# Cross-attention and mixture of experts: head stacks filled from tile to tile, the last residual added on TensorE, new due times

## The chip, the cores and the metric

The kernel runs on one core of one Trainium2 chip. The metric is the device time of one execution in microseconds. The median of three runs of the kernel before is 1670.79 us (1665.35 to 1675.45).

## The reference

Eight batches of 512 tokens, 512 features, 16 heads of 32. Layer norm, cross-attention to a context, a residual, a second layer norm, and a top-k mixture of eight experts in which each expert takes the 512 tokens with the highest probability for it. All in float32.

```python
def attn(q, k, v):                      # 8 x 512 x 512 each
    qh, kh, vh = heads(q @ Wq + bq), heads(k @ Wk + bk), heads(v @ Wv + bv)
    sim = einsum('bnid,bnjd->bnij', qh, kh) * 32 ** -0.5
    sim = where(mask, sim, lowest)
    return join(einsum('bnij,bnjd->bnid', softmax(sim), vh)) @ Wo + bo

x = x + attn(layernorm(x), ctx, ctx)
xf = layernorm(x).reshape(4096, 512)
route_prob = softmax(xf @ Ws + bs).T                 # 8 x 4096
route_vals, routes = top_k(route_prob, 512)
h = gelu(einsum('ekd,edf->ekf', xf[routes], W1) + b1)    # f = 2048
out = (einsum('ekf,efd->ekd', h, W2) + b2) * route_vals[..., None]
x = x + zeros.at[routes].add(out)
```

## The kernel before, in words

The attention part works on 32 groups g: batch b = g // 4 and four heads. Float32 products are made of fp32r ones, with every operand split into a hi and a lo half: hi·hi, lo·hi and hi·lo.

For a group, TensorE projects k and q: `proj` (L1855 to L1857), four times three matmuls for each of k and q, features on the partitions. ScalarE writes the hi half from PSUM (L1257, `qT_hi` or `kT_hi`, a tile of 128 partitions = 4 heads × 32 features, by 512 tokens), and VectorE the lo half (L1461).

The scores need another layout, the stack: 32 features of each head on partitions, the four heads side by side on the free axis, and hi, lo, hi (for q; hi, hi, lo for k) one under another, so that one matmul over 96 rows sums the three products. `kst` and `qst` are rings of NST = 3 stacks, a group uses slot g mod 3. The halves reach them through memory. SP issues `keep_hi` and `keep_lo` (L948, L955), each a store of 256 KB from the tile into `qk_rows`, and then `stack_hi` (L979, two transfers) and `stack_lo` (L990), which load it back as "(h d) s -> d h s". A stack's transfer waits for the store, and for the last score of group g − 3. The evacuation of the next projection, L1257 and L1461, waits for the store of the last. SP issues its transfers in one order of its own; a wait holds up all that stand behind it.

`max` (L1873) multiplies q by k for the row maxima, taken on VectorE (L1476), with the sum of exponentials on ScalarE (L1280). The maxima are transposed (`rows`, L1890) and become further rows of the stack (`by_row`, through POOL L1174). `score` (L1905) makes the scores once more, transposed, with the maxima subtracted; ScalarE exponentiates them into `p_ring` (L1292); `att` (L1916) multiplies by v, in fp32, four heads on 32 columns each. `rden` (L1897) and VectorE's L1508 divide; L1301 and L1532 split the result into `oT`.

For each tile t of 128 tokens of a batch, `outa` and `out` (L1932 to L1934) make the output projection of the first and the last two groups. In the last batch `out` is cut in two: `osum` with group 30, `out` with group 31, into the same bank. VectorE adds `outa` to x, then `out` (L1547), takes the statistics (L1380 to L1384), and normalises (L1389). `route` (L1944) transposes the result, `logits` (L1955) and `back` (L1963) make the router's values. From about 894 us the experts follow, which the change leaves alone.

Which step comes next on which engine is set before the program is written, by a planner (`attention_agenda`, class `Plan`). Every step has a due time (`at`, in groups; tables K_AT, Q_AT, MAX_AT, SPAN and others, plus LAG), a cost and the steps that must be ready. The planner plays the engines forward: on an engine, of the steps that can start within LOOK of the earliest, the one with the smallest due time goes. All seven general PSUM banks go by the same plan.

Of the kernel before, what the change touches and what calls it, by code (L numbers as in the profile page):

```python
# [371 lines left out]
LAG = {
    ("act", "proj"): 0.055, ("dve", "proj_lo"): 0.027, ("pool", "rows_lo"): -0.636, ("act", "rows"): 0.028, ("dve", "rows_lo"): -0.369,
    ("sync", "stack_hi"): -0.057, ("sync", "stack_lo"): 0.367, ("pool", "recip"): -0.231, ("dve", "rden"): -0.146, ("dve", "outa"): -0.826,
# [1776 lines left out]
```

## Time and profile before

| | before |
|---|---|
| median of three runs | 1670.79 us |
| the profiled execution | 1667.8 us |
| its span | 1666.0 us |
| mean granted clock of TensorE | 0.985 |
| TensorE busy (PE) | 1597.9 us, 96% |
| VectorE busy (DVE) | 1113.7 us, 67% |
| ScalarE busy (ACT) | 976.8 us, 59% |
| GpSimd busy (POOL) | 300.0 us, 18% |
| DMA, mean | 130 GB/s |

PE, DVE, ACT and POOL are TensorE, VectorE, ScalarE and GpSimd; SPq is SyncE's issue of transfers; PEld is the loading of weights, which runs beside PE. L1905 is line 1905 of the kernel. A row such as "out<-in" names what is written and what is read. The number in square brackets at a row's end is the time for which the engine stood idle before it, and what released it; "issue" is idle time for which the profile shows no wait. A matmul's own duration overlaps the next one's, so work is measured by the distance of the starts.

### The profile page before, as it was taken

The page shows a single profiled execution, that of the slowest core. Times are in us where ns is not written, and L with a number is a line of the kernel's source. Part 1 is how long each engine was busy: PE and PEld are TensorE (multiplying, and loading weights), DVE is VectorE, ACT ScalarE, POOL GpSimd, SP SyncE. Part 2 cuts the span into 40 slices and gives each one's busy share as a digit, 9 for nine tenths or more (in the row PEclk, how much of TensorE's full clock was granted, in tenths as well). Part 3 has the DMA queues.
Part 4 walks back from the last instruction along what each step waited for, and adds up shares of the span by engine and source line. Part 5 has one row for each costly group of instructions (what it writes and reads, how often), then busy time and mean ns, then how long its engine had stood idle before and what let it go on. Part 6 is the DMA issues. An engine that isn't in the chain of part 4 may idle for free.

```text
span 1666.0 us, 22367 instructions
## 1 busy us (share of the span) xinstructions
PE 1597.9 (96%) x7847; PEld 1162.0 (70%) x7847; DVE 1113.7 (67%) x1950; ACT 976.8 (59%) x2115; POOL 300.0 (18%) x396
## 2 busy tenths in 40 slices
PE   7999999999999999999886999999999999999997
PEld 5556666666666666666544787888888888888885
DVE  7676878878788797787746577765554555454543
ACT  5788898989989899798872223222222223232331
POOL 6220221302213022130300201002020202020110
PEclk9999999999999999999997999999999999999999
DMA  5643654626547364462611423416252524343330
GB/s 179 184 123 95 193 145 140 208 80 205 144 132 207 87 200 147 134 192 83 190 67 64 127 89 90 152 57 184 76 159 101 159 91 144 101 132 119 102 110 26
DMA packets 131271, 217.27 MB, mean 130 GB/s; under 512 B 17116, under 2 KB 51056, under 8 KB 131160
## 3 DMA queue, kind: packets, MB, share of 16 engines
q1 hardware_dynamic: 114520, 173.23, 33.1%
q0 software_dynamic: 16640, 42.61, 9.6%
q8 instruction: 63, 1.03, 0.3%
q14 instruction: 48, 0.39, 0.1%
HBM read 157.45 MB, written 57.82 MB: 129 GB/s over the span
## 4 chain that ended last, share of the span: by engine, by line
PE 86%; DVE 7%; ACT 2%; DMA 2%; issue 2%; POOL 0%; SPq 0%; DVEq 0%; POOLq 0%; ACTq 0%
PE ps_gen L888 9%; PE ps_gen L890 9%; PE ps_gen L889 9%; PE ps_gen L1905 7%; PE ps_gen L2069 7%; PE ps_gen L2071 7%; PE ps_gen L2070 7%; PE ps_gen L1873 7%; PE ps_att L1916 7%; PE ps_gen L1855 3%; PE ps_gen L1856 3%; PE ps_gen L1857 3%; PE ps_gen L1932 2%; PE ps_gen L1933 2%; PE ps_gen L1934 2%
## 5 line engine op out<-in xcount | busy, mean ns | idle before, releaser
L1476 DVE TENSOR_REDUCE nmax<-ps_gen 128x1 f32<-128x512 f32 x512 | 331.9, 684 | 79.5 <-PE ps_gen L1873 77.8
L1292 ACT ACTIVATE p_ring<-ps_gen,keep_scale 128x512 f32<-128x512 f32 x512 | 341.3, 702 | 44.2 <-PE ps_gen L1905 30.7
L1280 ACT ACTIVATE ps_gen<-ps_gen,nmax 128x512 f32<-128x512 f32 x512 | 342.6, 676 | 33.6 <-DVE nmax L1476 33.4
L1349 ACT ACTIVATE gel<-ps_gen,b_cols 128x512 f32<-128x512 f32 x128 | 88.3, 690 | 448.8 <-PE ps_gen L890 448.7
L1737 DVE TENSOR_TENSOR gel_lo<-gel,gel_hi 128x512 fp32r<-128x512 f32 x126 | 87.3, 692 | 281.6 <-ACT gel_hi L1350 277.3
L888 PE MATMUL ps_gen<-hT_hi,w_hi 128*128 128x512 f32 x512 | 202.2, 395 | 0.2 <-DVE hT_lo L1730 0.2
L1873 PE MATMUL ps_gen<-kst,qst 97*128 97x512 f32 x512 | 193.0, 424 | 8.6 <-issue 4.6
L890 PE MATMUL ps_gen<-hT_hi,w_lo 128*128 128x512 f32 x512 | 199.5, 390 | 0.0
L889 PE MATMUL ps_gen<-hT_lo,w_hi 128*128 128x512 f32 x512 | 199.4, 389 | 0.0
L1905 PE MATMUL ps_gen<-qst,kst 99*128 99x512 f32 x512 | 194.9, 424 | 3.8 <-DMA qst<-by_row 3.1
L2069 PE MATMUL ps_gen<-w_hi,gel_hi 128*128 128x512 f32 x504 | 198.1, 393 | 0.0
L2071 PE MATMUL ps_gen<-w_hi,gel_lo 128*128 128x512 f32 x504 | 196.5, 390 | 0.0
L2070 PE MATMUL ps_gen<-w_lo,gel_hi 128*128 128x512 f32 x504 | 196.3, 389 | 0.0
L1873 PEld LDWEIGHTS ps_gen<-kst,qst 97*128 97x128 f32 x512 | 95.4, 192 | 78.3 <-issue 50.0
L1905 PEld LDWEIGHTS ps_gen<-qst,kst 99*128 99x128 f32 x512 | 93.5, 190 | 78.2 <-issue 58.8
L1202 POOL DMA_INDIRECT out_x<-y_out,idx x28 | 49.6, 1770 | 511.1 <-ACT y_out L1369 504.7
L1916 PE MATMUL ps_att<-p_ring,v_sb 128*32 128x512 f32 x1024 | 138.4, 613 | 1.8 <-ACT p_ring L1292 1.6
L1280 ACT ACTIVATION_READ_ACCUMULATOR ps_gen<-ps_gen,nmax 128x1 f32 x512 | 113.8, 222 | 0.0
L890 PEld LDWEIGHTS ps_gen<-hT_hi,w_lo 128*128 128x128 f32 x512 | 96.1, 188 | 20.5
L888 PEld LDWEIGHTS ps_gen<-hT_hi,w_hi 128*128 128x128 f32 x512 | 96.1, 188 | 19.6 <-issue 0.5
L889 PEld LDWEIGHTS ps_gen<-hT_lo,w_hi 128*128 128x128 f32 x512 | 96.2, 188 | 19.3
L2071 PEld LDWEIGHTS ps_gen<-w_hi,gel_lo 128*128 128x128 f32 x504 | 94.6, 188 | 19.8
(218 smaller groups left out, 2672.0 us busy)
## 6 DMA issues: line engine op xcount, KB each, us to landing
w_raw<-in_L_ffn_W SPq DMA_DIRECT2D x128, 512.0 KB, 3.3
kst<-qk_rows SPq DMA_DIRECT2D x93, 256.0 KB, 4.0
qst<-qk_rows SPq DMA_DIRECT2D x93, 256.0 KB, 4.1
x_in<-in_x POOLq DMA_DIRECT2D x60, 256.0 KB, 4.1
out_x<-x_in SPq DMA_DIRECT2D x32, 256.0 KB, 3.3
qk_rows<-kT_hi SPq DMA_DIRECT2D x31, 256.0 KB, 2.3
qk_rows<-kT_lo SPq DMA_DIRECT2D x31, 256.0 KB, 3.7
qk_rows<-qT_hi SPq DMA_DIRECT2D x31, 256.0 KB, 2.0
```

The costliest lines, as they stand in the source:

```text
L888: e.matmul(psum, lhsT=wh, rhs=mh, start=(i == 0), stop=False)
L889: e.matmul(psum, lhsT=wh, rhs=ml, start=False, stop=False)
L890: last = e.matmul(psum, lhsT=wl, rhs=mh, start=False, stop=(i == n - 1))
L1280: e.activation(psum[:, :], psum[:, :], ACT.Exp, bias=nmax[g % 2][:, c], scale=-1.0, accum_out=den[g % 2][:, c]).then_inc(drained_sem("max" ...
L1292: e.activation(p_ring[n % NP_][:, :], ps("score", g, kt, h)[:, :], ACT.Exp, scale=keep_scale[:, b:b + 1]).then_inc(drained_sem("score", g, ...
L1476: e.tensor_reduce(nmax[g % 2][:, h * TB + t:h * TB + t + 1], ps("max", g, h, t)[:, :], AX.X, ALU.min).then_inc(s_min, 1)
L1873: e.matmul(ps("max", g, h, t)[:, :], lhsT=qst[k][0:ROWS_MAX, h, t * P:(t + 1) * P], rhs=kst[k][0:ROWS_MAX, h, :], start=True, stop=True).t ...
L1905: e.matmul(ps("score", g, kt, h)[:, :], lhsT=kst[k][0:ROWS_ALL, h, kt * P:(kt + 1) * P], rhs=qst[k][0:ROWS_ALL, h, :], start=True, stop=Tr ...
L1916: last = e.matmul(ps_att[h * DH:(h + 1) * DH, :], lhsT=v_sb[:, kt, (c4 * HG + h) * DH:(c4 * HG + h + 1) * DH], rhs=p_ring[((g * KT + kt) * ...
L2069: e.matmul(ps_y[tt], lhsT=gh, rhs=wh, start=(j == 0), stop=False)
L2070: e.matmul(ps_y[tt], lhsT=gh, rhs=wl, start=False, stop=False)
L2071: return e.matmul(ps_y[tt], lhsT=gl, rhs=wh, start=False, stop=(j == NF - 1))
```

## The change

Four things are changed.

- The stacks are filled from the tile itself: `keep_hi` and `keep_lo` are gone (124 stores of 256 KB), with `qk_rows`; `stack_hi` and `stack_lo` (now L963 and L974) read `qT_hi` and the others. For this the host permutes the columns of W_q and W_k and their biases, so that a tile's partition is 4·d + h and a stack's 32 × 4 rows are the tile's 128 partitions in order; the picks for group 0 are permuted alike. The evacuation of projection g (now L1244 and L1453) waits until the stack of g − 1 has landed.
- In the last batch the residual is added on TensorE: `osum` has one more matmul, the identity times `x_in` (L1937, fp32, 512 columns), behind `outa`'s addition. VectorE no longer adds there; statistics and norm read PSUM. ScalarE copies PSUM to `x_in` (L1294) for the store, and the norms of tiles 0 and 1 are written to `p_ring`.
- The planner knows a third number for a cost, the time that a transfer takes of the DMA engines, one after another.
- All due times, LOOK and LAG are other numbers, and so are some costs.

The core of the diff:

```diff
@@ planner
+            if part.wire:
+                wire_free = max(wire_free, start) + part.wire
+                part.ready = max(part.ready, wire_free + part.seen - part.wire)
-                self.add("keep_hi", w, g)
-                self.add("keep_lo", w, g)
-    "sync": {"keep_hi": (0.360, 2.30), "keep_lo": (0.360, 2.30), "stack_hi": (0.800, 6.00), "stack_lo": (0.400, 5.50),
+    "sync": {"stack_hi": (0.800, 3.80, 1.80), "stack_lo": (0.400, 3.30, 0.90), "mask_row": (0.400, 2.50, 0.10),
-LOOK = 0.048
+LOOK = 0.03778
-K_AT = ((0.297, 0.404), (-0.045, 0.294), (0.028, 0.08), (-0.316, 0.132))
+K_AT = ((0.27907, 0.32787), (-0.03226, 0.31951), (-0.28842, -0.05107), (-0.46132, -0.12707))
...
@@ SP, keep and stack
-                elif kind == "keep_hi":
-                    w, g = at
-                    if g > 2:
-                        on.wait_ge(s_stack_hi[w][(g - 2) % NST], 32 * stacked(g - 2))
-                    on.wait_ge(s_proj_hi[w], g + 1)
-                    e.dma_start(kept(w, g, 0), raw(qk[w, "hi"][:, :])).then_inc(s_kept_hi[w], 16)
...
-                    on.wait_ge(s_kept_hi[w], 16 * g)
+                    on.wait_ge(s_proj_hi[w], g + 1)
                     for r in ((0, 2) if w == "q" else (0, 1)):
-                        e.dma_start(raw(stack[r * DH:(r + 1) * DH, :, :]), kept_rows(w, g, 0)).then_inc(s_stack_hi[w][k], 16)
+                        e.dma_start(raw(stack[r * DH:(r + 1) * DH, :, :]), raw(qk[w, "hi"][:, :])).then_inc(s_stack_hi[w][k], 16)
...
-                    on.wait_ge(s_kept_lo[w], 16 * g)
+                    on.wait_ge(*drained("proj", w, g))
-                    e.dma_start(raw(stack[r * DH:(r + 1) * DH, :, :]), kept_rows(w, g, 1)).then_inc(s_stack_lo[w][k], 16)
+                    e.dma_start(raw(stack[r * DH:(r + 1) * DH, :, :]), raw(qk[w, "lo"][:, :])).then_inc(s_stack_lo[w][k], 16)
@@ ScalarE, proj; VectorE likewise with s_stack_lo
-                        on.wait_ge(s_kept_hi[w], 16 * (g - 1))
+                        on.wait_ge(s_stack_hi[w][(g - 1) % NST], 32 * stacked(g - 1))
@@ ScalarE, new
+                elif kind == "out" and at[0] == B - 1:
+                    on.wait_ge(s_ln, 3 * agenda.ln_turn["x1", b, t] + 1)
+                    e.activation(x_in[residual_slot(b, t)][:, :], ps("out", b, t)[:, :], ACT.Copy).then_inc(s_x1_kept, 1)
@@ VectorE, out
+                    if b < B - 1:
                         e.tensor_tensor(x1[:, :], ps("out", b, t)[:, :], x1[:, :], ALU.add).then_inc(drained_sem("out", b, t), 1)
                         statistics(("x1", b, t), x1[:, :])
+                    else:
+                        statistics(("x1", b, t), ps("out", b, t)[:, :])
@@ TensorE, osum
+                    if kind == "osum":
+                        on.wait_ge(*drained("outa", b, t))
+                        e.matmul(ps(*key)[:, :], lhsT=ident[:, :], rhs=x_in[residual_slot(b, t)][:, :], start=False, stop=False)
@@ host
+        if name in ('L0_xattn_Wq', 'L0_xattn_Wk', 'L0_xattn_bq', 'L0_xattn_bk'):
+            a = np.ascontiguousarray(a.reshape(-1, GB, HG, DH).transpose(0, 1, 3, 2).reshape(a.shape))
```

TensorE, up to the first max of the last group, the L1873 x3 at the end: L1873 is max, L1905 score, L1916 att, L1897 rden, L1890 the transpose of the maxima. The last matmul of the group's q projection stands ahead of the piece. Before, with two L1905 and three L1873 between it and the piece:

```order
L1916 MATMUL ps_att<-p_ring,v_sb 32x512 x4
L1905 MATMUL ps_gen<-qst,kst 128x512 x2
L1897 MATMUL ps_gen<-ident,rden_wide 128x128 x4
L1873 MATMUL ps_gen<-kst,qst 128x512 x2
L1905 MATMUL ps_gen<-qst,kst 128x512
L1873 MATMUL ps_gen<-kst,qst 128x512
L1905 MATMUL ps_gen<-qst,kst 128x512
L1916 MATMUL ps_att<-p_ring,v_sb 32x512 x4
L1873 MATMUL ps_gen<-kst,qst 128x512 x3
L1905 MATMUL ps_gen<-qst,kst 128x512 x2
L1890 MATMUL ps_gen<-ident,nmax 16x128
L1873 MATMUL ps_gen<-kst,qst 128x512 x3
```

After, with nothing between:

```order
L1873 MATMUL ps_gen<-kst,qst 128x512
L1905 MATMUL ps_gen<-qst,kst 128x512
L1873 MATMUL ps_gen<-kst,qst 128x512 x2
L1905 MATMUL ps_gen<-qst,kst 128x512
L1916 MATMUL ps_att<-p_ring,v_sb 32x512 x4
L1873 MATMUL ps_gen<-kst,qst 128x512
L1897 MATMUL ps_gen<-ident,rden_wide 128x128 x4
L1873 MATMUL ps_gen<-kst,qst 128x512
L1905 MATMUL ps_gen<-qst,kst 128x512
L1890 MATMUL ps_gen<-ident,nmax 16x128
L1905 MATMUL ps_gen<-qst,kst 128x512 x2
L1873 MATMUL ps_gen<-kst,qst 128x512 x3
```

Between the projection and the group's first max stand three L1905, four other L1873 and four L1916 fewer, so the max comes closer behind its projection.

TensorE, the end of the attention work: L1916 att, L1905 score, L1932 to L1934 an osum or out. Before:

```order
L1916 MATMUL ps_att<-p_ring,v_sb 32x512 x4
L1905 MATMUL ps_gen<-qst,kst 128x512 x2
L1916 MATMUL ps_att<-p_ring,v_sb 32x512 x4
L1932 MATMUL ps_gen<-wo_hi,oT_hi 128x512
L1933 MATMUL ps_gen<-wo_lo,oT_hi 128x512
L1934 MATMUL ps_gen<-wo_hi,oT_lo 128x512
```

After:

```order
L1916 MATMUL ps_att<-p_ring,v_sb 32x512 x4
L1905 MATMUL ps_gen<-qst,kst 128x512 x2
L1932 MATMUL ps_gen<-wo_hi,oT_hi 128x512
L1933 MATMUL ps_gen<-wo_lo,oT_hi 128x512
L1934 MATMUL ps_gen<-wo_hi,oT_lo 128x512
L1937 MATMUL ps_gen<-x_in,ident 128x512
L1916 MATMUL ps_att<-p_ring,v_sb 32x512 x4
L1932 MATMUL ps_gen<-wo_hi,oT_hi 128x512
L1933 MATMUL ps_gen<-wo_lo,oT_hi 128x512
L1934 MATMUL ps_gen<-wo_hi,oT_lo 128x512
L1937 MATMUL ps_gen<-x_in,ident 128x512
```

Two osum of three matmuls, which stood earlier, now stand among the last att, and every osum has the fourth matmul L1937 with the identity.

VectorE, from the last oT_lo on (L1532, now L1524). Before:

```order
L1532 SCALAR_TENSOR_TENSOR oT_lo<-att_n,bias_cols,oT_hi 128x512
L1547 TENSOR_TENSOR x_in<-ps_gen,x_in 128x512
L1380 BN_STATS stat<-x_in 128x6
L1382 BN_AGGR mv<-stat 128x2
L1384 TENSOR_SCALAR rstd<-mv 128x1
L1547 TENSOR_TENSOR x_in<-ps_gen,x_in 128x512
```

After:

```order
L1524 SCALAR_TENSOR_TENSOR oT_lo<-att_n,bias_cols,oT_hi 128x512
L1372 BN_STATS stat<-ps_gen 128x6
L1374 BN_AGGR mv<-stat 128x2
L1376 TENSOR_SCALAR rstd<-mv 128x1
L1372 BN_STATS stat<-ps_gen 128x6
L1374 BN_AGGR mv<-stat 128x2
L1376 TENSOR_SCALAR rstd<-mv 128x1
L1381 TENSOR_SCALAR p_ring<-ps_gen,mv,rstd 128x512
```

The addition L1547 is gone ahead of each tile's statistics, and the norm of tile 0 comes behind the statistics of tile 1.

## Rows read from the trace of the kernel before

**Rows 1.** The page, parts 1 and 4: TensorE's busy time; the chain by engine.
```profile
PE 1597.9 (96%) x7847; PEld 1162.0 (70%) x7847; DVE 1113.7 (67%) x1950; ACT 976.8 (59%) x2115; POOL 300.0 (18%) x396
...
PE 86%; DVE 7%; ACT 2%; DMA 2%; issue 2%; POOL 0%; SPq 0%; DVEq 0%; POOLq 0%; ACTq 0%
```

**Rows 2.** Stretches: us; busy of PE, PEld, DVE, ACT, POOL; clock; DMA share; GB/s.
```profile
80.00:85.00 5.00, 5.00 (x19) 2.57 (x18) 3.08 (x6) 2.83 (x8) 0.54 (x1) 0.53 0.94 255
200.00:300.00 100.00, 100.00 (x529) 65.52 (x528) 80.69 (x156) 91.28 (x213) 22.21 (x35) 1.00 0.51 149
830.00:835.00 5.00, 2.00 (x8) 1.10 (x12) 2.15 (x6) 3.76 (x11) 1.63 (x3) 0.72 1.06 306
855.00:875.00 20.00, 14.39 (x78) 6.38 (x74) 3.00 (x5) 13.23 (x22) 1.59 (x3) 1.00 0.00 1
```

**Rows 3.** TensorE in order of time, five places: start us, us, instruction, idle before.
```profile
78.03 1.19 PE L1873 MATMUL ps_gen<-kst,qst 97*128 97x512 f32 x2 [3.15 <-issue]
...
198.71 0.50 PE L1855 MATMUL ps_gen<-cT_hi,wk_hi 128*128 128x512 f32 x1 [0.55 <-DVE kT_lo L1461]
...
705.29 0.70 PE L1905 MATMUL ps_gen<-qst,kst 99*128 99x512 f32 x2 [1.71 <-DMA qst<-by_row]
...
833.27 1.62 PE L1873 MATMUL ps_gen<-kst,qst 97*128 97x512 f32 x3 [2.16 <-DMA qst<-qk_rows]
...
876.11 0.50 PE L1932 MATMUL ps_gen<-wo_hi,oT_hi 128*128 128x512 f32 x1 [2.36 <-DVE oT_lo L1532]
```

**Rows 4.** The chain of waits, near 65 and near 825: start us, us, what.
```profile
65.31 5.21 DMA qk_rows<-qT_hi
70.88 5.43 DMA qst<-qk_rows
...
823.54 3.65 DMA qk_rows<-qT_hi
828.04 5.03 DMA qst<-qk_rows
```

**Rows 5.** The page, part 6, transfers: KB each, us to landing.
```profile
qst<-qk_rows SPq DMA_DIRECT2D x93, 256.0 KB, 4.1
```

**Rows 6.** TensorE in order of time, 848.9 to 850.7.
```profile
848.94 0.39 PE L1934 MATMUL ps_gen<-wo_hi,oT_lo 128*128 128x512 f32 x1
849.16 0.63 PE L1905 MATMUL ps_gen<-qst,kst 99*128 99x512 f32 x2
849.72 1.07 PE L1916 MATMUL ps_att<-p_ring,v_sb 128*32 128x512 f32 x8
850.72 0.50 PE L1873 MATMUL ps_gen<-kst,qst 97*128 97x512 f32 x1
```

**Rows 7.** TensorE, ScalarE and VectorE around the projections of groups 2 and 31.
```profile
63.20 0.39 PE L1857 MATMUL ps_gen<-xT_hi,wq_lo 128*128 128x512 f32 x1
...
821.66 0.39 PE L1857 MATMUL ps_gen<-xT_hi,wq_lo 128*128 128x512 f32 x1
...
822.20 0.70 ACT L1257 ACTIVATE qT_hi<-ps_gen,bias_cols 128x512 fp32r<-128x512 f32 x1
...
823.99 0.74 DVE L1461 SCALAR_TENSOR_TENSOR qT_lo<-ps_gen,bias_cols,qT_hi 128x512 fp32r<-128x512 f32 x1
```

**Rows 8.** The chain of waits, the mark that each batch leaves.
```profile
503.36 1.80 DVE cT_lo L1412 x3
...
606.64 1.81 DVE cT_lo L1412 x3
...
713.19 1.80 DVE cT_lo L1412 x3
```

**Rows 9.** VectorE in the tail.
```profile
877.42 0.69 DVE L1547 TENSOR_TENSOR x_in<-ps_gen,x_in 128x512 f32<-128x512 f32 x1 [1.37 <-PE ps_gen L1934]
879.17 0.69 DVE L1547 TENSOR_TENSOR x_in<-ps_gen,x_in 128x512 f32<-128x512 f32 x1
886.29 0.55 DVE L1389 TENSOR_SCALAR hnT<-x_in,mv,rstd 128x512 f32<-128x512 f32 x1
```

More of the change, by code:

```diff
@@ L65, in __init__ @@
         self.engine, self.step, self.at = engine, step, at
-        self.busy, self.seen = cost
+        self.busy, self.seen, self.wire = cost if len(cost) == 3 else (*cost, 0.0)
         self.after, self.line = after, line
@@ L79, in __init__, with add @@
         self.lines = {}
-    def add(self, engine, step, at, after=(), line=None, takes=None, frees=None):
+    def add(self, engine, step, at, after=(), line=None, takes=None, frees=None, cost=None):
         line = (engine, line or step[0])
-        part = Part(engine, step, at + LAG.get(line, 0), COST[engine][step[0]], after, line, takes, frees)
+        part = Part(engine, step, at + LAG.get(line, 0), cost or COST[engine][step[0]], after, line, takes, frees)
         self.parts[(engine,) + step] = part
@@ L95, in run @@
         held = {}
+        wire_free = 0.0
         returned = {kind: [] for kind in HELD}
@@ L371 @@
+STATISTICS = (1.020, 1.10)
+LOOK = 0.03778
 HELD = {"max": 3, "score": 2}
 LAG = {
[L373 to L376 removed]
@@ L384 @@
-ROWS_AT, RECIP_AT, RDEN_AT, OSPLIT_AT, ATT_AT = -0.391, 0.334, 1.071, -0.392, 0.061
+    ("act", "proj"): 0.03482, ("dve", "proj_lo"): -0.00596, ("pool", "rows_lo"): -0.88337, ("act", "rows"): 0.04415, ("dve", "rows_lo"): -0.68861,
+    ("sync", "stack_hi"): 0.00369, ("sync", "stack_lo"): 0.48509, ("pool", "recip"): 0.06928, ("dve", "rden"): 0.02284, ("dve", "outa"): -0.87513,
+    ("dve", "csplit_lo"): 0.13813, ("dve", "turn_lo"): 0.02377, ("dve", "v"): 0.03864, ("dve", "out"): 0.13015, ("act", "turn"): 0.14026,
@@ new lines @@
+    ("dve", "back"): 0.05736, ("act", "osplit"): -0.10126, ("dve", "divide"): 0.15196, ("act", "logits"): -0.68145, ("pool", "add_bias"): -0.79753,
+    ("act", "csplit"): -0.46121, ("pe", "rows"): 0.33584, ("dve", "route"): -0.39133, ("dve", "max"): -0.06277, ("dve", "recip"): 0.4233,
+    ("act", "score"): 0.0286, ("act", "sum"): 0.01634, ("pe", "score"): -0.29535, ("dve", "osplit_lo"): 0.33544, ("sync", "den_in"): -0.36905,
+    ("sync", "den_out"): -0.3311, ("sync", "mask_row"): 0.30993, ("sync", "x1_norm"): -0.08373, ("sync", "out"): -0.06046,
+}
@@ L388 @@
-    "add_bias": (2, 1.633, 2.372), "outa": (2, 0.177, 1.039), "out": (4, 0.057, 0.784), "x1_norm": (4, 0.602, 1.176),
-    "route": (4, 0.403, 1.087), "logits": (4, 0.556, 1.139), "back": (4, 0.744, 1.133),
+    "v": (-1, 0.17009, 1.61709), "load_c": (-3, -0.00336, 0.19747), "csplit": (-3, -0.35517, 0.04247), "load_x": (-3, 0.64845, 0.65845),
+    "stats": (-3, 0.63203, 0.7478), "norm": (-3, 0.93933, 1.44351), "turn": (-3, 0.54053, 0.67893), "residual": (2, -0.06476, 0.50823),
+    "add_bias": (2, 1.66206, 1.75846), "outa": (2, 0.18862, 0.97992), "out": (4, 0.05675, 0.7842), "x1_norm": (4, 0.56895, 1.09159),
@@ L390 @@
+    "route": (4, 0.33815, 1.08473), "logits": (4, 0.37929, 0.93654), "back": (4, -0.13828, 0.84414),
 }
@@ L526, in attention_agenda @@
             if ends:
-                p.add("pe", ("osum", b, t), at("out"), [("dve", "osplit_lo", b * GB + 2)], takes=("out", b, t))
+                p.add("pe", ("osum", b, t), at("out"), [("dve", "osplit_lo", b * GB + 2), ("dve", "outa", b, t)], takes=("out", b, t))
             p.add("pe", ("out", b, t), at("out"), [("dve", "osplit_lo", b * GB + 3), ("pe", "osum", b, t)],
```

105 lines of the change are left out of this document (49 added, 56 removed).

## The prediction

> **What bounds the kernel now.** I read the page from its top. TensorE is busy for 1597.9 us of the span of 1666.0, and the chain that ended last is 86% TensorE, 7% VectorE, 2% ScalarE, 2% DMA and 2% issue [rows 1]. So only two things can save time: TensorE work that goes, and TensorE waits that go. The table by stretches shows where there are waits: in the steady part of attention (200:300) TensorE is busy 100.00 of 100 us, with ScalarE at 91.28 and VectorE at 80.69, while 830:835 holds 2.00 busy of 5, and 855:875 holds 14.39 of 20 [rows 2]. TensorE's own rows name the large waits [rows 3]: 3.15 us before 78.03 ("issue"), 0.55 before 198.71 (the K projection waits for a bank that VectorE's kT_lo gives back; six batches have this pair of 0.15 and 0.55), 1.71 before 705.29 (by_row), 2.16 before 833.27 (the query stack of the last group), 2.36 before 876.11 (the last oT_lo). The MoE stage behind 894 us is not touched; I cost it at nothing.
>
> The trace shows why 78.03 and 833.27 wait: on the chain stand "DMA qk_rows<-qT_hi" 5.21, then "DMA qst<-qk_rows" 5.43, and again 3.65 and 5.03 [rows 4]. A group's query stack goes through two transfers in a row, and the change takes one of them away.
>
> **Part A, the stack of group 2 (64 to 140 us).** The last q projection ends at 63.6 [rows 7]; the hi half is out of ScalarE at 65.3, where its first transfer starts [rows 4], and the lo half takes VectorE another 0.74 (the qT_lo of [rows 7]). Directly, the stack's transfers start near 66.3 and take 5.4 at most (the 5.43 of [rows 4], in the busiest DMA stretch), so the stack is whole at 71.7 to 72.5. Here and below I count TensorE's work between two places in the order, so many matmuls of each kind at the spacing of the trace (0.22 to 0.23 for an fp32r matmul, 1.00 for eight L1916, 0.1 for each change between the two, [rows 6]). Between the last q projection and the first max of group 2 it is 8.3 us instead of 11.3, so TensorE arrives at 71.9. The wait of 3.15 becomes 0 to 0.6: I take −2.5. Behind the old wait the granted clock is 0.53 in 80:85 [rows 2], the lower of the two levels (1.2 GHz); from 78.03 it lasts nearly to 85, and 6.5 us at half speed carry 3.25 of work, so a further −3.2 if the clock stays up. But ScalarE, with 2.83 of 5 busy there [rows 2], then has its own work for the same groups still to do and sets the pace behind it, so part comes back: I take half of it, +1.7. Sum −4.0; bounds −6.5 (nothing comes back) and −1 (the wait goes, the clock falls all the same and ScalarE takes the rest).
>
> **Part B, the steady batches (140 to 815).** Removed: 124 transfers of 256 KB and their rows on SP (573 become 449). TensorE did not wait for SP there, so the removal itself is worth nothing. What can be won are the waits: six times 0.70 at the K projection, −4.2, and the wait at 705.29. By the chain's marks the batch of 606.64 to 713.19 took 106.55 where the one before took 103.28 [rows 8], so this wait costs 3.3, not 1.7. In the new order the shortest stretch of TensorE work between the transpose of the max rows and the first score is 5.2 us, where it was 4.4; one event in seven batches at 4.4 makes it likelier than not that 5.2 covers it: −2.0 of 3.3. Against this stands what the new order adds. TensorE changes between fp32r and fp32 matmuls more often. The rows price a change [rows 6]: two score matmuls ahead of an fp32 block take 0.56 where the spacing alone, 0.22 to 0.23, gives 0.46, so 0.1, and I take as much for the way back. There are 260 blocks of fp32 work now where there were 239: 21 × 0.2 = 4.2 at most, 21 × 0.11 = 2.3 if part lies under weight loads; I take 2.3. Then the new wait: the evacuation of proj(g), ScalarE L1257 and VectorE L1461, waited until proj(g−1) had been stored, and now waits until stack(g−1) has landed, which in turn waits for the last score of g−4. Behind it on ScalarE stand exponentials, for which TensorE's banks wait. In the new order the q and k evacuations of successive groups lie some 25 us apart, so I price it at one hiccup of 0.15 per batch in seven, +1.0, plus +0.4 for the bank that one K projection per batch holds longer. Sum −4.2 − 2.0 + 2.3 + 1.0 + 0.4 = −2.5; bounds −8 and +6 (21 changes at 0.2, no wait gone, one 0.55 per batch more at the evacuations).
>
> Here is the place in which the shorter path matters in every batch. By the order, TensorE's work from the last q projection to the first max of the same group was 12.0 us at least and is now 8.7 at least (third group of a batch). What it must cover, from [rows 7]: the projection ends at 822.05; qT_hi runs to 822.90; qT_lo, held up by two maxima on VectorE, ends at 824.73; a transfer of 4.1 [rows 5] makes that 828.9, 6.9 us behind the projection. 8.7 covers 6.9 with 1.8 to spare. One could hope that the source in the chip's memory makes the transfer itself short. No row of before shows a tile-to-tile transfer; bounds are 3.65, the shortest here to hit the chain, and 5.43, the longest [rows 4]. I take 4.1.
>
> **Part C, the end of attention (815 to 876).** The 2.16 before 833.27 is the same double transfer: q projection ends 822.05, lo ready 824.73, stack at 828.9 to 830.2. The new order has only 4.3 us of TensorE work for it (7.2 before), so TensorE stands ready at 826.4 and then waits 2.5 to 3.8: the moved work is done later, so what counts is that the max starts at 829.6 instead of 833.3 with 2.9 us of other work left over. Net −0.8 for the wait, and the clock, 0.72 in 830:835 [rows 2], falls as before. Then the four osum get a matmul ident × x_in in fp32, 512 columns. The nearest row is a block of eight L1916 (two groups of four, each also 512 columns in fp32): 1.00 from 849.72 to 850.72 [rows 6], or 0.5 per four. Four 32-column ones may run side by side, so one full one is between 0.23 (an fp32r matmul) and 1.0; I take 1.0 with its changes. The last of the four falls in the 2.36 before 876.11; of the other three, two stand in stretches where ScalarE is the later engine (13.23 of 20 busy with the waits around it, [rows 2]) and cost little: +0.3 net (bounds −0.5, +4). Sum −0.5.
>
> The Trainium skill, "FP8 and Floating Point Precision", section "TensorE Precision Notes", says that true FP32 takes four passes through the array. With 0.23 for one pass, as an estimate, the matmul would be 0.92, four of them 3.7, and by that price alone this part would end at +3 if nothing hid them.
>
> **Part D, the tail (876 to 894).** VectorE sets the pace: from one L1547 (877.42) to the next (879.17) 1.75 per tile, of which the add itself is 0.69 [rows 9]. The add goes, 1.06 per tile stay, four tiles: −2.8, and the statistics start on the same matmul. The norm of tile 3 now reads PSUM and ends near 884.4 instead of 886.29 + 0.55 = 886.84. The ScalarE copies lie beside it; the norm waits for its tile's copy, but the statistics of the next tile cover that. With the route of tile 3 behind it I take −3.3 (that is a little over the adds, since TensorE's short waits between tiles go too; bounds −2.4, if the copy of tile 3 shows, and −3.6).
>
> **Sum.** −4.0 − 2.5 − 0.5 − 3.3 = −10.3. Against the profiled execution (1667.8) that is 1657.5; this execution stands 3.0 below the median of 1670.79, by which it would be 1660.5. I say 1659.
>
> **Rivals.**
> *No change worth the name.* TensorE is at 100.00 of 100 in the steady part [rows 2], so there is nothing to win there; what is gained in A come back where ScalarE is late, the 21 changes and the ident matmuls eat the rest: −1 + 0.5 + 0 − 2.4, about −3, 1665 to 1668. For it: 91.28 of ScalarE. Against it: the tail's −2.4 is certain and the 3.15 is not ScalarE's.
> *Slower: the stack lands late in every batch.* Place: the first max of each batch's third group, which has 8.7 us of cover. It decides when landing exceeds 5.9 us, or 5.3 with ScalarE one exponential (0.6) later than in [rows 7]. One such event costs what 705.29 did, 3.3 [rows 8]; times seven is +22.9, and with A and D kept and B's K waits gone, 1667.8 + 22.9 + 2.3 − 4.2 − 4.0 − 0.5 − 3.3 = 1681. For it: 5.03 and 5.43 in [rows 4]. Against: both fall where DMA engines are loaded to 1.06 and 0.94 [rows 2]; the steady share is 0.51, and the change takes traffic away.
> *A larger gain.* All waits of A and B go and the clock stays up: −6.5 − 6 − 1 − 3.6 = −17, 1651.
> *The new due times do not match the chip* (waits as at 705.29 turn up at other places, one or two): this is the no-change case with 3.3 to 6.6 more, 1664 to 1671.
>
> **How the numbers follow.** Half a per cent, 8.35 us, is what a measurement of this kernel tells from no change. Forecast 0.50 (it is faster in 0.42, within the bound in 0.08, as B's upper half brings it there); no change, with the mismatched due times, 0.27 (0.24 within, 0.03 slower); larger gain 0.15; slower by late stacks 0.08. So faster 0.57, same 0.32, slower 0.11. The range leaves out the slower case and the far end of the larger gain: 1648 to 1672.
>
> **What would show it.** In the changed profile: "DMA qst<-qT_hi" at 3.7 to 4.5 us with no transfer ahead of it (wrong above 5.3); PE idle before the first max near 72 under 0.7 and no stretch of low clock behind it; the batch period at or below 103.3; PE busy up by 2 to 6 us; L1937 at 1.0 or below; TensorE still waits 2.5 or more for the last group's stack near 827 to 830; in the tail 1.0 per tile on VectorE. The forecast is wrong if the batch period grows over 103.8, or if PE rows show a wait for qst or kst in every batch.

## The result and the profile after

The changed kernel takes 1730.51 us (median of 4 runs, 1728.29 to 1735.74) against 1669.07 us before (4 runs): the ratio is 1.0372, interval 1.0357 to 1.0388. It is 61 us slower; I had forecast 10 faster.

The experts are not touched and take what they took: from the first matmul L1975 (956.76) to the end of the span 771.6 us, before 771.7 from L1972 (894.29). All the loss, 62.5 us in the profiled execution, lies ahead of them.

The page of the changed kernel: span and TensorE, the queue of the hardware transfers, the chain by engine, and the transfers that fill the stacks (KB each, us to landing).

```profile
PE 1621.2 (94%) x7855; PEld 1168.5 (68%) x7855; DVE 1111.0 (64%) x1946; ACT 979.8 (57%) x2119; POOL 299.7 (17%) x396
...
q1 hardware_dynamic: 96664, 140.71, 34.8%
...
PE 73%; DMA 8%; ACT 8%; DVE 7%; issue 3%; SPq 0%; POOL 0%; ACTq 0%; DVEq 0%; POOLq 0%
...
kst<-kT_hi SPq DMA_DIRECT2D x62, 256.0 KB, 5.6
qst<-qT_hi SPq DMA_DIRECT2D x62, 256.0 KB, 5.6
...
kst<-kT_lo SPq DMA_DIRECT2D x31, 256.0 KB, 6.6
qst<-qT_lo SPq DMA_DIRECT2D x31, 256.0 KB, 7.4
```

TensorE's share of the chain fell from 86% to 73%, and DMA rose from 2% to 8% [rows 1]. A stack's transfer lands 5.6 us (hi) and 6.6 to 7.4 us (lo) after its issue, where it took 4.1 from memory [rows 5]. The queue moved 140.7 MB in 34.8% of the engines' time; before it moved 173.2 MB in 33.1%.

TensorE in order of time at three places; the first is the max of group 2, which had 3.15 in [rows 3], the others are of a kind that now comes in every batch.

```profile
76.73 1.62 PE L1873 MATMUL ps_gen<-kst,qst 97*128 97x512 f32 x3 [4.03 <-DMA qst<-qT_hi]
...
333.19 0.40 PE L1857 MATMUL ps_gen<-cT_hi,wk_lo 128*128 128x512 f32 x1
338.26 0.76 PE L1873 MATMUL ps_gen<-kst,qst 97*128 97x512 f32 x1 [4.67 <-issue]
...
451.79 0.77 PE L1873 MATMUL ps_gen<-kst,qst 97*128 97x512 f32 x1 [6.17 <-issue]
```

There are seven such waits (226.32, 338.26, 451.79, 562.24, 672.14, 786.36, 897.25), each before the first max of a batch's fourth group, 3.5 to 6.2 us long; an eighth, of 2.60, stands before 107.60, where the fourth group of the first batch begins. The mean distance between the seven is 111.8 us; a batch took 103.3 before [rows 8]. 8.5 us times seven is 60.

SP's issues ahead of the wait at 338.26, in order of time, and of the chain that ends in it two pieces (start us, us, what):

```profile
324.23 1.21 SPq L963 DMA_DIRECT2D kst<-kT_hi  x2
325.48 0.63 SPq L974 DMA_DIRECT2D kst<-kT_lo  x1
327.92 1.19 SPq L963 DMA_DIRECT2D qst<-qT_hi  x2
329.16 0.61 SPq L974 DMA_DIRECT2D qst<-qT_lo  x1
```

```profile
328.51 8.18 DMA qst<-qT_hi
...
338.26 0.76 PE ps_gen L1873
```

Six transfers of 256 KB stand in a row, three for k from 324.23 and three for q from 327.92, and the max starts 14.0 us after the first issue. The chain names a hi transfer of 8.18, which ends at 336.69; the last one issued is qT_lo, and the chain doesn't show when it landed.

Stretches of the changed kernel, and last a batch of the kernel before: us; busy of PE, PEld, DVE, ACT, POOL; clock; DMA share; GB/s.

```profile
330.00:335.00 5.00, 3.59 (x22) 2.12 (x14) 3.92 (x11) 4.63 (x12) 2.28 (x4) 1.00 1.08 166
335.00:340.00 5.00, 1.74 (x6) 0.70 (x10) 0.94 (x2) 0.51 (x1) 0.00 (x0) 0.78 0.27 40
340.00:345.00 5.00, 5.00 (x26) 3.39 (x19) 3.32 (x7) 2.75 (x7) 1.12 (x2) 0.54 0.19 52
226.32:338.26 111.94, 106.01 (x536) 68.30 (x537) 83.57 (x161) 94.40 (x221) 22.95 (x36) 0.97 0.55 105
338.26:451.79 113.53, 106.28 (x536) 68.67 (x537) 83.54 (x161) 94.39 (x221) 22.73 (x36) 0.97 0.54 104
451.79:562.24 110.45, 105.81 (x536) 68.33 (x537) 83.55 (x161) 94.38 (x221) 22.75 (x36) 0.98 0.54 106
...
503.36:606.64 103.28, 102.57 (x540) 67.01 (x536) 83.57 (x162) 94.50 (x223) 22.73 (x36) 1.00 0.53 155
```

In 330:335 the DMA engines are fully loaded (1.08) and move 166 GB/s; before, at 1.06, they moved 306 [rows 2]. The second line shows TensorE idle, the third the granted clock at 0.54, the lower level, after it. The next three lines are three batches: 112.0 us on average, with TensorE busy for 106.0; the batch before had 103.3 and 102.6. So of the 8.7 us that a batch is longer, 5.3 are idle time and 3.4 are longer work. e5 below, in the same due times with hardly a wait and the clock at 1.00, has 1.2 of the 3.4; the other 2.2 come with the half clock behind each wait, an estimate by that difference.

### The profile page after: what moved, and what is told of

The parts are those of the page before. It is cut to its first block, busy times and chain, and to the rows that moved or that the text cites. A ratio compares the mean times of both kernels' runs of the same rounds, so it can differ in the third digit from the quotient of the medians.

```text
span 1728.4 us, 22149 instructions
## 1 busy us (share of the span) xinstructions
PE 1621.2 (94%) x7855; PEld 1168.5 (68%) x7855; DVE 1111.0 (64%) x1946; ACT 979.8 (57%) x2119; POOL 299.7 (17%) x396
## 3 DMA queue, kind: packets, MB, share of 16 engines
q1 hardware_dynamic: 96664, 140.71, 34.8%
## 4 chain that ended last, share of the span: by engine, by line
PE 73%; DMA 8%; ACT 8%; DVE 7%; issue 3%; SPq 0%; POOL 0%; ACTq 0%; DVEq 0%; POOLq 0%
PE ps_gen L886 8%; PE ps_gen L887 8%; PE ps_gen L888 8%; PE ps_gen L2072 7%; PE ps_gen L2074 7%; PE ps_gen L2073 7%; PE ps_att L1916 5%; PE ps_gen L1905 5%; PE ps_gen L1873 5%; DMA qst<-qT_hi 3%; ACT ps_gen L1267 3%; ACT p_ring L1279 2%; DMA out_x<-x_in 2%; DVE nmax L1468 2%; PE ps_gen L1855 2%
## 5 line engine op out<-in xcount | busy, mean ns | idle before, releaser
L1279 ACT ACTIVATE p_ring<-ps_gen,keep_scale 128x512 f32<-128x512 f32 x512 | 344.8, 704 | 96.4 <-PE ps_gen L1905 71.9
L1267 ACT ACTIVATE ps_gen<-ps_gen,nmax 128x512 f32<-128x512 f32 x512 | 345.8, 682 | 45.5 <-DVE nmax L1468 45.3
L1873 PE MATMUL ps_gen<-kst,qst 97*128 97x512 f32 x512 | 196.3, 427 | 49.4 <-issue 36.3
L1905 PE MATMUL ps_gen<-qst,kst 99*128 99x512 f32 x512 | 203.8, 438 | 9.0 <-DMA qst<-by_row 5.9
L1905 PEld LDWEIGHTS ps_gen<-qst,kst 99*128 99x128 f32 x512 | 96.6, 196 | 101.7 <-issue 71.4
L1873 PEld LDWEIGHTS ps_gen<-kst,qst 97*128 97x128 f32 x512 | 96.5, 194 | 96.1 <-issue 63.3
L1916 PE MATMUL ps_att<-p_ring,v_sb 128*32 128x512 f32 x1024 | 144.9, 640 | 2.6 <-ACT p_ring L1279 2.6
L1267 ACT ACTIVATION_READ_ACCUMULATOR ps_gen<-ps_gen,nmax 128x1 f32 x512 | 117.0, 229 | 0.0
```

The costliest lines, as they stand in the source:

```text
L1267: e.activation(psum[:, :], psum[:, :], ACT.Exp, bias=nmax[g % 2][:, c], scale=-1.0, accum_out=den[g % 2][:, c]).then_inc(drained_sem("max" ...
L1279: e.activation(p_ring[n % NP_][:, :], ps("score", g, kt, h)[:, :], ACT.Exp, scale=keep_scale[:, b:b + 1]).then_inc(drained_sem("score", g, ...
L1873: e.matmul(ps("max", g, h, t)[:, :], lhsT=qst[k][0:ROWS_MAX, h, t * P:(t + 1) * P], rhs=kst[k][0:ROWS_MAX, h, :], start=True, stop=True).t ...
L1905: e.matmul(ps("score", g, kt, h)[:, :], lhsT=kst[k][0:ROWS_ALL, h, kt * P:(kt + 1) * P], rhs=qst[k][0:ROWS_ALL, h, :], start=True, stop=Tr ...
L1916: last = e.matmul(ps_att[h * DH:(h + 1) * DH, :], lhsT=v_sb[:, kt, (c4 * HG + h) * DH:(c4 * HG + h + 1) * DH], rhs=p_ring[((g * KT + kt) * ...
```

## The experiments

**e1, transfers alone.** SP alone, six of 256 KB in a row, then a wait for all:

```python
go(by_mem[i // 3][r*32:(r+1)*32, :, :], rows[i*P:(i+1)*P, :].rearrange("(h d) s -> d h s", d=32))
go(by_tile[i // 3][r*32:(r+1)*32, :, :], src[:, :])      # 128 partitions x 512
go(by_head[i // 3][r*32:(r+1)*32, h, :], src[h*32:(h+1)*32, :])   # 64 KB, four each
go(one[k][0:32, :, :], ...)                              # one alone, from memory, from the tile
go(wide[:, i, :], src[:, :]);  go(widm[:, i, :], rows[i*P:(i+1)*P, :])
```

> This kernel computes nothing of the reference: SP alone moves 256 KB pieces, six in a row of each kind, and waits for all six before the next kind; the whole sequence comes twice, then a tile is stored 32 times into the output. Theory R (rate): a transfer from a tile of 128 partitions to 32 partitions x 4 rows runs at a lower rate than the same one from memory; the profile of the changed kernel shows 160 to 175 GB/s with the DMA engines at 0.98 to 0.99. Six by_tile pieces (1.57 MB) then take 9.0 to 9.8 us and 1.5 to 2 more to the last landing, six by_mem pieces 7.2 us and the same. Theory S (the source does not matter, 32 partitions at the destination set the rate): both 7.2 and 2. Tile to tile with 128 partitions on both sides (wide) tells whether a tile as source is slow by itself: 9 us or more if it is, near 4 if the 32 partitions are needed for it. One alone: R 3.2 to 3.7 by tile against 2.8 to 3.2 from memory; S no difference.

SP in order of time (the next kind starts when the last has landed), and the median landings:

```profile
3.45 2.71 SPq L41 DMA_DIRECT2D by_mem<-in_x  x6
12.27 3.94 SPq L41 DMA_DIRECT2D by_tile<-src  x6
26.57 15.15 SPq L41 DMA_DIRECT2D by_head<-src  x24
43.17 0.32 SPq L41 DMA_DIRECT2D one<-in_x  x1
49.93 3.77 SPq L41 DMA_DIRECT2D wide<-src  x6
55.73 2.73 SPq L41 DMA_DIRECT2D widm<-in_x  x6
```

```profile
by_mem<-in_x SPq DMA_DIRECT2D x12, 256.0 KB, 4.8
by_tile<-src SPq DMA_DIRECT2D x12, 256.0 KB, 7.7
...
wide<-src SPq DMA_DIRECT2D x12, 256.0 KB, 2.5
...
one<-in_x SPq DMA_DIRECT2D x2, 256.0 KB, 2.8
one<-src SPq DMA_DIRECT2D x2, 256.0 KB, 3.9
```

By_mem takes 8.8 us (3.45 to 12.27), by_tile 14.3 (to 26.57), wide 5.8. Less one alone (2.8 from memory, 3.9 from the tile; for wide its median landing, 2.5) and over five, a further transfer costs 1.20 us from memory, 2.08 from the tile into 32 partitions, and 0.66 from tile to tile with 128 partitions on both sides: 218, 126 and 397 GB/s. The 397 is a lower bound, since SP took 3.77 us to issue the six, 0.63 each. Theory R holds in direction and S falls; the size is beyond R, which had 11.8 us at most where 14.3 were measured. And the tile as a source isn't slow by itself: wide is the fastest of all. By_head was held by SP's issues (15.15 us for 24), so its rate wasn't seen.

**e8, transfers again,** with the row order and the pattern taken apart:

```python
go(mem[...], rows[i*P:(i+1)*P, :].rearrange("(d h) s -> d h s", h=4))      # by_mem, the tile's order
go(hed[...][r*32:(r+1)*32, h, :], src[h*32:(h+1)*32, :])   # by_head, h = 0, 1 on SP, 2, 3 on ScalarE
go(nar[...][r*32:(r+1)*32, :, :], wide[0:32, 0:4, :])      # narrow
go(hlf[...][r*32+16*k:r*32+16*k+16, :, :], src[64*k:64*k+64, :])           # halves
```

> Transfers alone again, nothing of the reference is computed. by_tile as before (six of 256 KB from 128 partitions to 32 partitions x 4 rows, partition 4d + h to row h of partition d), by_mem from memory rows in that same order, by_head four pieces of 64 KB each that keep the partition's number modulo 32 (half of them on ScalarE's queue), narrow from 32 partitions x 4 rows to 32 partitions x 4 rows, halves 128 KB each. If what is slow is that four source partitions go into one (the pattern), by_head and narrow take 7 to 9 us for 1.57 MB and by_tile 12 again; if any tile as source is slow into 32 partitions, narrow takes 12 as well; if the order of rows were it, by_mem would now take 12 and not 8.8.

```profile
7.84 3.88 SPq L44 DMA_DIRECT2D by_tile<-src  x6
22.11 2.68 SPq L44 DMA_DIRECT2D by_mem<-in_x  x6
31.23 7.90 SPq L44 DMA_DIRECT2D by_head<-src  x12
40.61 5.79 SPq L44 DMA_DIRECT2D narrow<-wide  x6
50.03 7.64 SPq L44 DMA_DIRECT2D halves<-src  x12
```

By_tile 14.3 again, by_mem in the tile's row order 9.1, narrow 9.4, by_head 9.4 (7.9 of it issuing), halves 14.6 (50.03 to 64.59). Narrow has the tile as its source and by_mem the order of rows, and neither is slow. Slow is the pattern in which, within one transfer, four neighbouring partitions of the source go into the four rows of one partition. By_head brings four source partitions into each partition too, but in four transfers, on two queues and held by their issue, so it doesn't tell which part of the pattern does it. Why the chip is slow there, no run tells.

**e2, the direct path in the old order.**

```diff
+                elif kind in ("keep_hi", "keep_lo"):
+                    pass
-                    on.wait_ge(s_kept_hi[w], 16 * g)
+                    on.wait_ge(s_proj_hi[w], g + 1)
-  kept_rows(w, g, 0)
+  raw(qk[w, "hi"][:, :])
-                        on.wait_ge(s_kept_hi[w], 16 * (g - 1))
+                        on.wait_ge(s_stack_hi[w][(g - 1) % NST], 32 * stacked(g - 1))
```

> The kernel before with its own planner, costs and due times, where only the way into the stacks is changed: keep_hi and keep_lo issue nothing, the stacks are filled from the tiles, the evacuations wait for the stacks, the host permutes the columns. TensorE's, ScalarE's and VectorE's orders are those of before. Theory R (the transfers themselves are what is slow): slower than before, 1685 to 1725, with waits of 1 us and more for qst or kst, though fewer than in the changed kernel since the old order leaves 12 us and not 8.7 between a projection and its max. Theory T (the new due times are what is slow): within 5 us of before, 1664 to 1674.

1677.09 us, ratio 1.0044 (1.0029 to 1.0059): slower, but by 7 us, not by the 15 to 55 of theory R, and outside the 1664 to 1674 of T as well. One batch of it (columns as above):

```profile
510.18:615.13 104.95, 102.69 (x540) 67.10 (x536) 83.65 (x162) 94.51 (x223) 22.81 (x36) 1.00 0.58 112
```

A batch takes 104.9, 1.6 more than before, with TensorE busy as long (102.7). The transfers land as late as in the changed kernel (5.6 us for hi, 6.7 and 6.8 for lo), and in the old order they cost little. The longest wait for them is 4.28 us, before the first max of the last group.

**e3, the new order with memory as the source.**

```diff
+            rows = qk_rows["qk".index(w), part]
+            if g == 1:
+                e.dma_start(rows, raw(qk[w, ("hi", "lo")[part]][:, :])).then_inc(s_once[w, part], 16)
+                e.wait_ge(s_once[w, part], 16)
-  e.dma_start(raw(stack[r * DH:(r + 1) * DH, :, :]), raw(qk[w, "hi"][:, :]))
+  e.dma_start(raw(stack[r * DH:(r + 1) * DH, :, :]), rows)
```

> The changed kernel, the same order on every engine and the same waits, but the stacks of groups 2 to 31 are read from memory, where the tiles of group 1 were stored once; so from group 2 on the scores are those of wrong rows (the stacks hold group 1's q and k), and no store stands in the path. Theory R: the time of the late stacks goes: 1652 to 1670, landing near 4, no wait over 1 us for a stack in the steady part. Theory T: it stays near the changed kernel, 1715 to 1735. Theory S (source makes no difference, the new waits of the evacuations are the cause): 1715 to 1735 too, with landings of 5.6 to 7 as in the changed kernel.

1679.57, ratio 1.0061 (1.0043 to 1.008). 51 of the 61 us go with the source alone, on the same order and the same waits. It stays over the 1652 to 1670 of R; a wait of 1.1 to 2.0 remains at the same place of every batch, of which this is one:

```profile
421.99 0.47 PE L1882 MATMUL ps_gen<-kst,qst 97*128 97x512 f32 x1 [1.56 <-issue]
```

So even with landings of 4.1 to 4.3 us the new order leaves too little ahead of that max. Taken with e2: the slow transfers in the old order cost 7 us, the new order with transfers from memory 10, both together 61. The loss is that the two meet.

**e4, the new due times on the old path** (LOOK, LAG, K_AT, Q_AT, MAX_AT, the single ones and SPAN exchanged, nothing else).

> The kernel before with the stacks through memory and the residual on VectorE as before; only LOOK, LAG and all due times (K_AT, Q_AT, MAX_AT, SPAN and the single ones) are those of the changed kernel. Theory R: the due times are not the cause, but they were not chosen for this path, so 1668 to 1690. Theory T: 1710 or more.

1697.94, ratio 1.0154 (1.012 to 1.0187), between the two theories' ranges: 28 us slower. TensorE waits 24.8 us in eight stretches ahead of a max (L1873). So the due times do harm on the path through memory too, with the costs of before.

**e5, the costs mended.** The planner's two rows, and nothing else of the changed kernel:

```diff
-    "sync": {"stack_hi": (0.800, 3.80, 1.80), "stack_lo": (0.400, 3.30, 0.90),
+    "sync": {"stack_hi": (1.200, 6.00, 4.10), "stack_lo": (0.600, 3.90, 2.05),
```

> The changed kernel with two rows of the planner's costs set to what its trace measured: stack_hi (0.8, 3.8, 1.8) becomes (1.2, 6.0, 4.1) and stack_lo (0.4, 3.3, 0.9) becomes (0.6, 3.9, 2.05), so that a transfer takes 2.05 us of the DMA engines in the plan and not 0.9. All due times stay. The order then leaves 14.2 us of TensorE work or more between every q projection and its first max from group 5 on, 13.1 for group 2, where the changed kernel had 8.7 and 8.3. Theory P (the plan believed in faster transfers and put the k and q stacks of one group per batch in a row right ahead of the max): the batch period falls from 112 to 103.5 to 105, and the kernel to 1655 to 1675. Rival T (the new due times are bad whatever the transfers cost): 1690 or more. Rival E (the evacuations that now wait for the landed stack stop ScalarE): waits of TensorE for ps_gen and p_ring rise, 1680 to 1700.

1674.35, ratio 1.003 (1.002 to 1.0039). These two rows give back 56 of the 61 us, and it is still 5 us slower than before. The largest wait for a max in a steady batch is now this one, and a batch:

```profile
513.29 0.49 PE L1873 MATMUL ps_gen<-kst,qst 97*128 97x512 f32 x1 [0.53 <-ACT ps_gen L1267]
```

```profile
408.45:513.29 104.84, 103.82 (x536) 66.93 (x536) 83.43 (x162) 94.58 (x222) 22.98 (x36) 1.00 0.60 112
```

P holds, T and E fall. 104.8 per batch, 103.8 of it busy: 1.2 more work than before's 102.6. Its order has 32 blocks of fp32 matmuls in a batch, before 30; at 0.2 each that explains 0.4, and the rest is open.

**e9, one due time earlier.**

```diff
-Q_AT = ((0.41811, 0.43411), (0.4161, 0.43104), (0.19844, 0.6128), (0.27018, 0.45154))
+Q_AT = ((0.41811, 0.43411), (0.2161, 0.23104), (0.19844, 0.6128), (0.27018, 0.45154))
```

> The changed kernel with one due time moved: Q_AT[1], the q projection of the fourth group of every batch, from (0.4161, 0.43104) to (0.2161, 0.23104). In the order its last q projection then stands 10.8 us of TensorE work ahead of the group's first max and no longer 8.7, but the k projection, 13.9 ahead before, now ends 9.4 ahead. Theory Q (what counts is that the six transfers of k and q, 12.3 us at 2.05 each, must all be through, whichever comes last): from the first of the two projections, 10.8 ahead, 1.3 for the evacuation and 12.3 + 2 for the transfers, so late by 5 us or more, as in the changed kernel or worse: 1715 to 1740. Rival L (the late landing belongs to q's own three transfers, distance 8.7 against 10.8): the wait of 4 to 6 us shrinks by 2.1 and with it the half clock, 1695 to 1712.

1747.26, ratio 1.0467 (1.045 to 1.0484): slower still, though the q projection stands 2.1 us further ahead, and over both ranges. Now q's three go first and k's come last, and TensorE waits for kT_lo, as Q has it:

```profile
431.30 1.21 SPq L963 DMA_DIRECT2D qst<-qT_hi  x2
...
436.64 0.55 SPq L974 DMA_DIRECT2D kst<-kT_lo  x1
```

```profile
448.21 0.47 PE L1873 MATMUL ps_gen<-kst,qst 97*128 97x512 f32 x1 [1.81 <-DMA kst<-kT_lo]
```

From the first issue of the six to the max it is 16.9 us. But the wait itself is 1.5 to 2.4 us in the six steady batches, shorter than the 3.5 to 6.2 of the changed kernel and than Q's 5. What makes the kernel slower are waits at other places: by the table of waits, 12.2 us for banks that L1267 gives back (3.0 in the changed kernel), 9.9 for qT_lo (1.6) and 9.5 for the maxima ahead of L1890 (0.7). So e9 shows that k's transfers count as well as q's, and that moving one due time opens new waits; it doesn't confirm Q's price. Rival L, with 1695 to 1712, falls.

**e6, the residual alone** (before, with the hunks of the diff on osum, out, x1_norm, route, L1294 and their rows in the planner).

> The kernel before, stacks through memory and old due times, with only the second part of the change: in the last batch the residual is added by a matmul with the identity, statistics and norm read PSUM, ScalarE copies. Theory D (the tail's terms as predicted, 3.3 saved and 0.3 paid): 2 to 4 us faster than before, ratio 0.9976 to 0.9988, one matmul L1937 near 0.9 to 1.0 us. Rival: the copy and the norm that waits for it lie on the path, no difference or up to 2 us slower.

1666.61, ratio 0.9992 (0.9978 to 1.0005). The medians lie 2.2 us apart, but the ratio is nearer to 1 than the 0.9976 to 0.9988 expected, and its interval doesn't tell it from nothing.

**e7, two stacks direct,** with e6's change:

```diff
+DIRECT = {("q", 2), ("q", NG - 1)}
-                    on.wait_ge(s_kept_hi[w], 16 * g)
+                    now = (w, g) in DIRECT
+                    on.wait_ge(*((s_proj_hi[w], g + 1) if now else (s_kept_hi[w], kept_no(w, g))))
-  kept_rows(w, g, 0)
+  raw(qk[w, "hi"][:, :]) if now else kept_rows(w, g, 0)
```

> e6 and, beside it, the query stacks of groups 2 and 31 alone filled from the tile; all others go through memory. Theory: where the double transfer was on the chain the direct one saves what the transfer is shorter by: before 5.21 + 0.35 + 5.43 behind qT_hi for group 2, now some 8 (three transfers at 2.05 and 2 more), so 2 to 3 us at 78 us and, for group 31, 827.9 + 5.0 becomes 824.7 + 7 = 831.7, 1 us. Together with e6 5 to 9 us faster than before, ratio 0.9945 to 0.997. Rival: at these places the K stack's transfers are in the way and nothing is saved, ratio of e6.

1664.37, ratio 0.9973 (0.9962 to 0.9984): the one version that is clearly faster than before, by 4.5 us, a little short of the 5 to 9 expected. The first max of group 2 and of group 31:

```profile
76.42 0.71 PE L1905 MATMUL ps_gen<-kst,qst 97*128 97x512 f32 x2 [1.76 <-DMA qst<-qT_hi]
...
828.38 1.62 PE L1905 MATMUL ps_gen<-kst,qst 97*128 97x512 f32 x3 [1.35 <-DMA qst<-qT_lo]
```

The waits are 1.76 and 1.35, where [rows 3] had 3.15 and 2.16 and e6 has 3.62 and 2.54.

**e10, four direct** (DIRECT also holds ("k", 2) and ("k", NG - 1)).

> As e7 (through memory everywhere but for groups 2 and 31, residual on TensorE), but k's stacks of groups 2 and 31 are filled directly too. Theory: k's landing is not what TensorE waits for there, while its three direct transfers take 2.05 and not 1.2 us each and stand ahead of q's: 0 to 2.5 us slower than e7, ratio to before 0.997 to 0.999. Rival: the two stores and the SP rows that go make room: 0.995 to 0.9965.

1672.8, ratio 1.0026 (1.0015 to 1.0037): 8.4 us above e7, outside what either side expected. At both places six slow transfers now stand in a row:

```profile
78.61 0.47 PE L1905 MATMUL ps_gen<-kst,qst 97*128 97x512 f32 x1 [3.37 <-issue]
...
840.15 1.62 PE L1905 MATMUL ps_gen<-kst,qst 97*128 97x512 f32 x3 [4.91 <-DMA qst<-qT_lo]
```

**e11, old due times with the mended costs** (e5 with LOOK, LAG and all due times of before).

> The kernel of e5 (all stacks direct, residual on TensorE, costs of the transfers as measured) with LOOK, LAG and all due times of the kernel before. The planner's order has 10.4 us of TensorE work at least between a q projection and its max. Theory: with the transfers' true price in the plan either set of due times gives nearly the same, within 6 us of e5, 1668 to 1684. Rival T (the new due times are the worse ones): 3 to 8 us faster than e5, under 1671.

1707.83, ratio 1.0245 (1.0224 to 1.0265): a miss, for the theory and for rival T. Neither set of due times is better by itself: with the mended costs the old ones take 33 us more than the new ones (e5), and on the old path with the old costs the new ones take 28 more than the old (e4). Three batches of e11 (413.65 to 746.00) take 109.5 to 112.3 with the clock at 0.97 to 0.98 and waits for hnT, p_ring and ps_gen; which due time does it wasn't tried.

## Why the prediction was wrong

**The step that failed** is in part B: "8.7 covers 6.9 with 1.8 to spare." Three things in it were off.

- *The landing.* I took 4.1, with 5.43 as the upper bound, both from transfers out of memory. It was 5.6 for hi and 7.4 for lo. The row that had to be bounded, a tile-to-tile transfer, was not in the trace, and I bounded it by rows of another source. Rows with the same destination and another source gave no bound.
- *The queue.* I counted q's three transfers from q's own evacuation. In the new order k's three are issued 3.7 us ahead of them, and what must fit is all six: 5 × 2.08 + 3.9 = 14.3 by e1, 14.0 in the trace. I had the distances of both projections from the order, and used q's alone. In e9, with q further away and k nearer, it is k's last transfer that TensorE waits for.
- *ScalarE.* In [rows 7] qT_hi started 0.15 after the projection's end; here the projection ended at 324.0 and qT_hi was on ScalarE from 327.10:

```profile
327.10 0.80 ACT L1244 ACTIVATE qT_hi<-ps_gen,bias_cols 128x512 fp32r<-128x512 f32 x1
```

Five exponentials stood ahead of it.

Together, at this max: qT_lo was ready 4.8 us behind the projection (328.82) and not 2.7, and the max came 9.4 us behind that and not 4.1. The 6.9 became 14.3; TensorE's other work covered 9.6 (to 333.59), and the rest is the wait of 4.67.

**The rival was right in mechanism** and sign, and had 0.08. I called the place the third group of a batch; it is the fourth, the third counted from group 1. Its price was wrong too: 3.3 per event, from 705.29, gave 1681. Measured are 8.5 per batch, since the wait itself is 4.7 on average and not 1.7. The point from which it decides, a landing over 5.9, fits as well: lo lands at 6.6 to 7.4. What I should have done is to price that point: with a margin of 1.8 us on a term of 4.1 that no row showed, 0.08 was too low, and the range had to reach it.

**The Trainium skill's rule.** "SBUF — State Buffer", section "Door 1: The DMA port swizzle (why [64,N] ≈ [32,N])", says that 32 partitions reach half the ports, about 218 GB/s. For a source in memory e1 agrees, 218 GB/s; for the tile it measured 126. So the rule is a ceiling that this pattern doesn't reach, and the measurement decides. I had drawn from it that the source makes no difference, which the page doesn't say.

**Part A.** The first max of group 2 came at 76.73 instead of 78.03, after a wait of 4.03: the shorter path gave 1.3 of the 4.0 there. With the wait still in place the granted clock fell as well, to 0.68 in 76 to 95. Then came waits of 2.60 (before 107.60) and, for by_row, of 3.72 (before 116.45); the largest by_row wait there before was 1.25.

**Part B's other terms.** The 0.55 for kT_lo is gone from TensorE's waits, as forecast. The by_row wait of 705.29, which I had more likely gone than not, is there with 2.13 before 760.16. The changes between fp32 and fp32r were priced at 0.11 for each block; e5's 1.2 us per batch may say that this was low, but two blocks more explain 0.4 at most, so this stays open.

**Part C.** One matmul L1937 takes 0.95 us, where I took 1.0 (from its start to the next instruction's; the profile has two records for each fp32 matmul, eight for the four L1937):

```profile
937.50 1.02 PE L1937 MATMUL ps_gen<-x_in,ident 128*128 128x512 f32 x2
938.45 1.07 PE L1916 MATMUL ps_att<-p_ring,v_sb 128*32 128x512 f32 x8
```

The Trainium skill, "FP8 and Floating Point Precision", section "TensorE Precision Notes", says four passes, from which I had 0.92 as an estimate; the trace agrees. By the same two records, the eight L1916 of [rows 6] are one group of four heads and not two, so four take 1.0 and not 0.5, as much as one full matmul. The row set no price below 1.0; the 1.0 that I took held. The wait for the last group's stack, forecast at 2.5 to 3.8, was 6.17, before 897.25.

**Part D** was right. VectorE in the tail, and TensorE's first matmul of it and of the experts:

```profile
941.07 0.75 DVE L1524 SCALAR_TENSOR_TENSOR oT_lo<-att_n,bias_cols,oT_hi 128x512 fp32r<-128x512 f32 x1 [0.79 <-ACT oT_hi L1288]
942.88 0.70 DVE L1372 BATCH_NORM_STATS2 stat<-ps_gen 128x6 f32<-128x512 f32 x1 [1.06 <-PE ps_gen L1934]
...
943.90 0.69 DVE L1372 BATCH_NORM_STATS2 stat<-ps_gen 128x6 f32<-128x512 f32 x1
...
949.41 0.81 DVE L1381 TENSOR_SCALAR hnT<-ps_gen,mv,rstd 128x512 f32<-128x512 f32 x1 [0.18 <-ACT x_in L1294]
...
941.87 0.50 PE L1932 MATMUL ps_gen<-wo_hi,oT_hi 128*128 128x512 f32 x1 [0.61 <-DVE oT_lo L1524]
...
956.76 0.53 PE L1975 MATMUL ps_gen<-ind,ones_h 128*128 128x112 bf16 x4 [2.93 <-DVE ind L1610]
```

From the end of the last oT_lo to the start of L1610, whose result TensorE's first matmul of the experts waits for, it took 17.46 before (876.05 to 893.51) and takes 14.17 now (941.82 to 955.99), −3.29 where −3.3 was forecast. The first two statistics follow each other at 1.02 where [rows 9] had 1.75 per tile (the later ones, from 945.65 on, have a norm between them); the norm reads PSUM and takes 0.81, 0.26 more than the 0.55 there, which I had not foreseen. In the kernel's time the part could not be told from nothing by itself (e6).

## What to carry to other kernels

A transfer that the trace doesn't show is not bounded by one with another source: six of them in a kernel of their own price it. Count, ahead of a wait, all transfers that share the DMA engines, from the first one's issue and not from the last one's. Due times don't carry over to another path or other costs unmeasured: they lost 28 us in e4 and 39 in e11. When a path is changed, measure its price first, since two wrong rows of costs were worth 56 us here.

## What the runs showed of the hardware

- 256 KB from the four partitions 4d to 4d + 3 into four rows of partition d cost 2.08 us each in a row (126 GB/s); the same bytes from memory 1.20 (218), between tiles of 128 partitions 0.66 at most (397 GB/s and over). In the changed kernel the DMA engines moved 166 GB/s at a share of 1.08, where 306 went through at 1.06 before.
- SP takes 0.6 us to issue each of them (1.21 for a pair), and 0.32 for one from memory alone, 0.45 each for six in a row (2.71).
- A TENSOR_SCALAR of 128 × 512 on VectorE took 0.81 us with PSUM as its source and 0.55 with the tile.
